# Gathering one operand by accumulating transfers, with two queues trading their loads, in a two-layer adapter kernel

## The chip, the cores and the metric

One Trainium2 chip (trn2), one core. The metric is the device time of one execution in microseconds (us); the figure of a kernel is the median of its runs.

## The reference

32 samples of x, each 64 x 512. Two residual layers follow each other, both conditioned by an index per sample:

```python
def _L0_cond_ref(x, conditions, weights):      # weights: 200 x 64 x 64
    w = weights[conditions]
    return jnp.einsum('bct,bcd->bdt', x, w)

def _L1_cond_ref(x, W, A, Bm, scalings, adapter_idx):   # W 512x512, A 8x16x512, Bm 8x512x16
    H = jnp.einsum('btd,od->bto', x, W)
    xa = jnp.einsum('btd,brd->btr', x, A[adapter_idx])
    delta = jnp.einsum('btr,bor->bto', xa, Bm[adapter_idx])
    return H + delta * scalings[adapter_idx][:, None, None]

x = x + _L0_cond_ref(x, itok_B_1_198, L0_cond_weights)
x = x + _L1_cond_ref(x, L1_cond_W, L1_cond_A, L1_cond_Bm, L1_cond_scalings, itok_B_0_6)
```

All of it is float32.

## The kernel before, in words

Two samples share the 128 partitions, so there are 16 tiles of 128 x 512. For each tile the kernel applies layer 1 first, on the raw x: z = x (W + identity), and beside it u = x A for the two samples of the tile. Layer 0 and its residual are then one product with w0 + identity, where w0 is a 128 x 128 block-diagonal matrix with the two samples' 64 x 64 weights. The low-rank part is v = u (w0 + identity), then v B, added in the same PSUM bank.

The columns of a tile's first product are W's 512 and A's 32 (2 samples x rank 16), 544 in all, split into two PSUM banks of 272. The W bank holds W columns alone, the A bank the other W columns and the 32 of A. Each operand is split into a rounded high part (ScalarE, fp32r) and a low part (VectorE, the difference), and a bank is twelve matmuls: high x high, low x x high, and high x x low W, for each of four blocks of K (`PRODUCTS`, `products`). Tiles 0 and 1 (`PLAIN = 2`) don't do that: their banks are plain fp32 products of unrounded operands, four for a bank (`plain_products`), recorded as two matmuls each. Their A columns are copied by ScalarE, scaled, into both ends of `w_late` (`take_raw_a`, `RAW_A`). For later tiles all eight adapters' A are scaled once, rounded and split into `a_table`, and GpSimd casts the two samples' columns from it into `moving` (`take_a`): even tiles at one end, odd tiles at the other.

Each engine has its order of work written out by hand; engines wait for each other through semaphores only. The queues before the change are:

- SyncE (SP): the index list, head_b, head_d, w_late, then for each tile x (`load_x`), the two 64 x 64 blocks of w0 (`load_w0`, 16 KB each, line 232) and, from tile 6 on, the store of the tile six before.
- GpSimd: the identity, a memset of all of `w0_sb` (line 302), then B's rows for each tile (`load_b`, line 290: two transfers of 128 KB, each row of B to four partitions, waiting for the buffer four tiles before), an addition of the identity to w0 (`add_identity`, line 299; one tile at a time for tiles 0 and 1, later two tiles at once, at odd tiles), and `take_a` (line 283).
- ScalarE: head_a, head_c and a_scales are asked for; then high parts of W, x, z, B, v and w0, the copies of z for tiles 0 and 1 and the copies of the output. `high_of_w0` (line 400) for tiles 2 and 3 stands between `take_z(1, A_PART)` and `high_of_v(1)`.
- VectorE: the identity's additions to W's diagonal, then the low parts and the mask of u by sample (`take_low_rank`).
- TensorE: the W banks of tiles 0 and 1, W bank of tile 2 in between, A bank of tile 0, `weigh_low_rank(0)` (v, line 685), A bank of tile 1, `plain_layer0(0)` (line 702 and the B product, line 696), `weigh_low_rank(1)`, A bank of tile 2, `plain_layer0(1)`, `weigh_low_rank(2)` (line 688), and from tile 3 on a loop: A bank, two thirds of the W bank, layer 0 of the tile before (lines 709, 710, 696, 714), v, and the last third of the W bank.

In the profile w0_sb and w0_parts are shown as w_sb and w_parts.

Of the kernel before, what the change touches and what calls it, by code (L numbers as in the profile page):

```python
# [6 lines left out]
def adapted_residual_kernel(nc, xt, heads, w0, head_a, head_b, head_c, head_d, w_late_t, a_t, b_t, out):  # L7
# [20 lines left out]
    GROUPS = 4  # L28
# [22 lines left out]
    RAW_A = (AC + LATE, 0)  # L51


    HH, HL, LH = 0, 1, 2
    PRODUCTS = [(n, k) for n in (HH, LH, HL) for k in range(K)]

# [13 lines left out]
            (HEAD_AT[3] + X_HALF, HEAD_AT[3] + 2 * X_HALF))  # L70

# [11 lines left out]
    with ctx:  # L83
# [14 lines left out]
        head = sb("head", [P, HEAD_AT[-1]], fp32)  # L98
        w_late = sb("w_late", [P, K, AC + LATE + AC], fp32)
# [37 lines left out]
        w0_cleared = sem("w0_cleared")  # L137
# [13 lines left out]
        w0_added = sem("w0_added")  # L151
# [27 lines left out]

        def x_block(t, k):  # L180

            at = X_AT[t][k // (K // 2)] + k % (K // 2) * P
            return head[:, at:at + P]

        def x_of(t):

            return head[:, X_AT[t][0]:X_AT[t][0] + WIDTH] if t < EARLY else x_raw[:, t - EARLY, :]

        def w_rows(p):

            (c0, _), (k0, k1) = PIECES[p]
            if c0:
                return w_late[:, k0:k1, AC:AC + LATE]
            return head[:, W_AT[p]:W_AT[p] + 2 * HALF].rearrange("p (k n) -> p k n", k=K // 2)

        def w_block(k, c0, c1):

            if c0 >= HALF:
                return w_late[:, k, AC + c0 - HALF:AC + c1 - HALF]
# [18 lines left out]
        def z_part(t, part):  # L218
            bank = bank_of(t, part)
            at, col, n = Z_PARTS[side(t)][bank]  # L220
            if t < PLAIN and part == A_PART and RAW_A[t] == 0:
                at += AC
# [3 lines left out]
        def _(sync):  # L226
# [3 lines left out]
            def load_w0(which, t):  # L230
                for s in range(PER):
                    sync.dma_start(w0_sb[s * C:(s + 1) * C, t, s * C:(s + 1) * C],
                                   w0[ds(which[s], 1), :, :].rearrange("a c d -> (a c) d"),
                                   ).then_inc(w0_loaded[BATCH_OF[t]], 16)
# [9 lines left out]
            sync.dma_start(w_late[:, :, AC:AC + LATE], w_late_t).then_inc(w_late_loaded, 16)  # L244
            sync.wait_ge(index_loaded, 16)
            which = read_indices(sync, 0, 0, w0.shape[0], 2 * READ)
            sync.wait_ge(w0_cleared, 1)
            load_w0(which[0], 0)
            load_w0(which[1], 1)
            load_x(3)  # L250
            load_w0(which[2], 2)
            load_w0(which[3], 3)
            for t in range(4, TILES):
                if t % READ == 0:
                    which = read_indices(sync, 0, t, w0.shape[0], READ)
                load_x(t)
                load_w0(which[t % READ], t)
# [11 lines left out]
        def _(pool):  # L269
# [5 lines left out]
            def take_a(which, t):  # L275

                at = 0 if t % 2 else AC + OUT
# [7 lines left out]
            def load_b(which, t):  # L285

                if t >= BBUFS:
                    pool.wait_ge(b_stack_ready, t - BBUFS + 1)
                for s in range(PER):
                    pool.dma_start(b_raw[s * C:(s + 1) * C, t % BBUFS, :],  # L290
                                   b_t[ds(which[s], 1), :, :].rearrange("a r (g n) -> (a r) g n", g=1)
                                   .to_broadcast([RANK, GROUPS, OUT]),
                                   ).then_inc(b_loaded[t % BBUFS], 16)

            def add_identity(i):
                first, end = BATCHES[i]
                pool.wait_ge(w0_loaded[i], 16 * PER * (end - first))
                every = ident[:].rearrange("p (a q) -> p a q", a=1).to_broadcast([P, end - first, P])
                nc.gpsimd.tensor_tensor(out=w0_sb[:, first:end, :], in0=w0_sb[:, first:end, :], in1=every,  # L299
                                        op=ALU.add).then_inc(w0_added, 1)  # L300
# [25 lines left out]
        def _(act):  # L326
# [5 lines left out]
            first = read_indices(act, 1, 0, ADAPTERS, PLAIN)  # L332
# [13 lines left out]
            def take_raw_a(t):  # L346

                at = RAW_A[t]
# [34 lines left out]
            def high_of_x(t):  # L383
                act.wait_ge(x_loaded[t - 2], 16)
                if t >= PLAIN + XBUFS:
                    act.wait_ge(w_bank_done, t - XBUFS + 1)
                nc.scalar.activation(x_high[:, t % XBUFS, :], x_of(t), ACT.Copy).then_inc(x_high_ready, 1)  # L387
# [9 lines left out]
            def high_of_w0(i):  # L397
                first, end = BATCHES[i]
                act.wait_ge(w0_added, i + 1)
# [429 lines left out]
```

## Time and profile before

| | |
|---|---|
| time, median of 3 runs | 76.97 us (76.96 to 77.12) |
| the profiled execution | 76.68 us, of which 75.0 are the span |
| granted TensorE clock | 1.00, the 2.4 GHz level |
| TensorE (PE) busy | 70.7 us, 94% |
| weight loads (PEld) | 65.4 us, 87% |
| VectorE (DVE) busy | 55.2 us, 74% |
| ScalarE (ACT) busy | 51.3 us, 68% |
| GpSimd (POOL) busy | 32.8 us, 44% |
| DMA | 14.55 MB, mean 194 GB/s over the span |

Times are counted from the start of the span. L12 is line 12 of the kernel. Register work, branches and the issuing of transfers by SP and ACT are not counted as busy; the time in which GpSimd makes the descriptors of its transfers is. Matmuls overlap, and the end of one is modelled; the chain that ended last gives each only the time by which it moved the chain on.

### The profile page before, as it was taken

The page shows a single profiled execution, that of the slowest core. Times are in us where ns is not written, and L with a number is a line of the kernel's source. Part 1 is how long each engine was busy: PE and PEld are TensorE (multiplying, and loading weights), DVE is VectorE, ACT ScalarE, POOL GpSimd, SP SyncE. Part 2 cuts the span into 40 slices and gives each one's busy share as a digit, 9 for nine tenths or more (in the row PEclk, how much of TensorE's full clock was granted, in tenths as well). Part 3 has the DMA queues.
Part 4 walks back from the last instruction along what each step waited for, and adds up shares of the span by engine and source line. Part 5 has one row for each costly group of instructions (what it writes and reads, how often), then busy time and mean ns, then how long its engine had stood idle before and what let it go on. Part 6 is the DMA issues. An engine that isn't in the chain of part 4 may idle for free.

```text
span 75.0 us, 1943 instructions
## 1 busy us (share of the span) xinstructions
PE 70.7 (94%) x468; PEld 65.4 (87%) x468; DVE 55.2 (74%) x143; ACT 51.3 (68%) x126; POOL 32.8 (44%) x76
## 2 busy tenths in 40 slices
PE   5999899999999999999999999999999999999940
PEld 5996689786999999999999999999999999999930
DVE  3019499897989877979797959797797949765920
ACT  0733888957988686977668666867696867566440
POOL 5700399997846282556245620690258320000000
PEclk9999999999999999999999999999999999999999
DMA  0999378786678757978968675578326430303025
GB/s 0 290 389 380 87 227 231 209 253 194 187 246 285 254 166 234 253 217 294 334 211 294 223 261 143 141 212 282 120 62 220 140 144 0 140 13 140 0 100 179
DMA packets 9677, 14.55 MB, mean 194 GB/s; under 512 B 3650, under 2 KB 4418, under 8 KB 9666
## 3 DMA queue, kind: packets, MB, share of 16 engines
q1 hardware_dynamic: 7554, 9.16, 37.5%
q0 software_dynamic: 1536, 4.20, 18.4%
q10 hardware_dynamic: 576, 1.07, 4.1%
q8 instruction: 4, 0.07, 0.4%
q14 instruction: 7, 0.06, 0.3%
HBM read 10.23 MB, written 4.19 MB: 192 GB/s over the span
## 4 chain that ended last, share of the span: by engine, by line
PE 86%; DMA 8%; SPq 1%; DVE 1%; issue 0%
PE z_ps L654 56%; DMA head<-head_d 8%; PE z_ps L642 6%; PE out_ps L696 5%; PE out_ps L709 4%; PE out_ps L710 4%; PE out_ps L714 4%; PE v_ps L688 2%; PE out_ps L702 2%; DVE out_sb L629 1%; PE v_ps L685 1%; SPq L242 0%; SPq L241 0%; PE v_ps L714 0%; PE v_ps L710 0%
## 5 line engine op out<-in xcount | busy, mean ns | idle before, releaser
L654 PE MATMUL z_ps<-moving,x_high 128*128 128x272 f32 x224 | 33.2, 288 | 0.0
L654 PEld LDWEIGHTS z_ps<-moving,x_high 128*128 128x128 f32 x224 | 29.8, 188 | 0.7 <-ACT z_plain L373 0.2
L290 POOL DMA_DIRECT2D b_raw<-b_t x32 | 16.2, 508 | 14.4 <-DMA a_scales<-a_t 5.4
L654 PE MATMUL z_ps<-moving,x_low 128*128 128x272 f32 x112 | 18.8, 289 | 0.0
L654 PEld LDWEIGHTS z_ps<-moving,x_low 128*128 128x128 f32 x112 | 15.8, 188 | 0.1
L511 DVE TENSOR_TENSOR z_low<-z_ps,z_high 128x272 fp32r<-128x272 f32 (+1 forms) x28 | 11.8, 422 | 1.2 <-ACT z_high L364 0.2
L283 POOL CAST moving<-a_table 128x128 fp32r x28 | 8.0, 316 | 10.5 <-PE z_ps L654 10.5
L520 DVE TENSOR_TENSOR b_stack<-b_raw,b_high 128x512 fp32r<-128x512 f32 x16 | 11.5, 718 | 0.4 <-ACT b_high L380 0.4
L380 ACT ACTIVATE b_high<-b_raw,group_sb 128x512 fp32r<-128x512 f32 x16 | 11.5, 716 | 0.0
L394 ACT ACTIVATE v_high<-v_ps,group_sb 128x128 fp32r<-128x128 f32 x16 | 5.9, 366 | 7.8 <-PE v_ps L688 7.8
L364 ACT ACTIVATE z_high<-z_ps 128x272 fp32r<-128x272 f32 (+1 forms) x28 | 10.5, 376 | 0.5 <-PE z_ps L654 0.3
L488 DVE TENSOR_TENSOR x_low<-x_raw,x_high 128x512 fp32r<-128x512 f32 x13 | 9.8, 757 | 0.1
L413 ACT ACTIVATE out_sb<-out_ps 128x512 f32<-128x512 f32 x15 | 8.8, 590 | 0.5 <-PE out_ps L714 0.5
L387 ACT ACTIVATE x_high<-x_raw 128x512 fp32r<-128x512 f32 x13 | 8.3, 637 | 0.0
L409 ACT ACTIVATE low_rank_parts<-own_low_rank 128x96 fp32r<-128x96 f32 x14 | 4.0, 284 | 5.9 <-DVE own_low_rank L540 5.9
L299 POOL TENSOR_TENSOR w_sb<-w_sb,ident 128x256 f32<-128x256 f32 (+1 forms) x9 | 6.9, 769 | 2.5 <-DMA w_sb<-w 2.4
L696 PE MATMUL out_ps<-b_stack,v_stack 128*128 128x512 f32 (+1 forms) x16 | 7.0, 435 | 0.0
L546 DVE TENSOR_TENSOR low_rank_parts<-own_low_rank,low_rank_parts 128x32 fp32r<-128x32 f32 x14 | 3.2, 227 | 4.9 <-ACT low_rank_parts L409 4.9
L709 PE MATMUL out_ps<-z_high,w_parts 128*128 128x512 f32 (+1 forms) x14 | 5.4, 388 | 0.0
L710 PE MATMUL out_ps<-z_high,w_parts 128*128 128x512 f32 (+1 forms) x14 | 5.4, 383 | 0.0
L714 PE MATMUL out_ps<-z_low,w_parts 128*128 128x512 f32 (+1 forms) x14 | 5.4, 382 | 0.0
L560 DVE SCALAR_TENSOR_TENSOR v_stack<-v_ps,group_sb,v_rest 128x128 fp32r<-128x128 f32 x14 | 4.9, 351 | 0.5
(58 smaller groups left out, 77.1 us busy)
## 6 DMA issues: line engine op xcount, KB each, us to landing
b_raw<-b_t POOLq DMA_DIRECT2D x32, 128.0 KB, 3.2
out<-out_sb SPq DMA_DIRECT2D x15, 256.0 KB, 3.2
x_raw<-xt SPq DMA_DIRECT2D x13, 256.0 KB, 3.7
w_sb<-w SPq DMA_DIRECT2D x32, 16.0 KB, 3.2
w_late<-w_late_t SPq DMA_DIRECT2D x1, 480.0 KB, 6.9
head<-head_c ACTq DMA_DIRECT2D x1, 400.0 KB, 4.2
head<-head_d SPq DMA_DIRECT2D x1, 384.0 KB, 6.1
head<-head_a ACTq DMA_DIRECT2D x1, 264.0 KB, 2.9
```

What stands on the lines that cost most here:

```text
L290: pool.dma_start(b_raw[s * C:(s + 1) * C, t % BBUFS, :], b_t[ds(which[s], 1), :, :].rearrange("a r (g n) -> (a r) g n", g=1) .to_broadcast ...
L364: nc.scalar.activation(z_high[:, t % 2, col:col + n], z, ACT.Copy).then_inc(z_high_ready[part], 1)
L380: nc.scalar.activation(b_high[:, t % 2, :], b_raw[:, t % BBUFS, :], ACT.Copy, scale=group_sb[:, LOW_B:LOW_B + 1]).then_inc(b_high_ready, 1)
L413: nc.scalar.activation(out_sb[:, t, :], out_ps[t % 2][:], ACT.Copy).then_inc(out_ready, 1)
L488: nc.vector.tensor_tensor(out=x_low[:, t % XBUFS, :], in0=x_of(t), in1=x_high[:, t % XBUFS, :].bitcast(fp32), op=ALU.subtract).then_inc(x_ ...
L511: nc.vector.tensor_tensor(out=z_low[:, t % 2, col:col + n], in0=z, in1=z_high[:, t % 2, col:col + n].bitcast(fp32), op=ALU.subtract).then_ ...
L520: nc.vector.tensor_tensor(out=b_stack[:, t % 2, :], in0=b_raw[:, t % BBUFS, :], in1=b_high[:, t % 2, :].bitcast(fp32), op=ALU.subtract).th ...
L654: last = nc.tensor.matmul(z_bank(t, part), x[:, t % XBUFS, k * P:(k + 1) * P], moving[:, int(n == HL), k, at:at + HALF], start=((n, k) == ...
L696: return nc.tensor.matmul(dst, v_stack[:, t % 2, :], b_stack[:, t % 2, col:col + n], start=False, stop=stop)
L709: nc.tensor.matmul(dst, w0_parts[:, t, 0, :], z_high[:, t % 2, col:col + n], start=True, stop=False)
L710: nc.tensor.matmul(dst, w0_parts[:, t, 1, :], z_high[:, t % 2, col:col + n], start=False, stop=False)
L714: return nc.tensor.matmul(dst, w0_parts[:, t, 0, :], z_low[:, t % 2, col:col + n], start=False, stop=True)
```

## The change

- w0 is no longer cleared, loaded by SyncE and then increased by the identity on GpSimd. VectorE copies the identity into all of `w0_sb` at the start (two instructions, `w0_preset`), and GpSimd asks for transfers that add w0's blocks to it (`add_w0`, `accum_op=ALU.add`), for tiles 4 and up two tiles at once, at even tiles. Waits for `w0_added` become waits for the transfers (`w0_loaded`).
- B's rows are asked for by SyncE (`load_b` moved), with x of tile 4 ahead of B of tile 3.
- Tile 1's A bank is computed from rounded parts: x tile 1 is rounded and split (`high_of_x(1)`, `low_of_x(1)`), GpSimd casts its A columns from `a_table` (`take_a` of tile 1), and the bank is twelve matmuls with the low part of x last (`LOW_X_LAST`). `a_table` is made ahead of W's last two pieces, and tile 2's `take_a` waits for tile 1's bank, since both use the same columns.
- VectorE and ScalarE get a new order around it.

```diff
         @block.sync
-            which = read_indices(sync, 0, 0, w0.shape[0], 2 * READ)
-            sync.wait_ge(w0_cleared, 1)
-            load_w0(which[0], 0)
-            load_w0(which[1], 1)
+            which = read_indices(sync, 1, 0, ADAPTERS, 2 * READ)
+            load_b(which[0], 0)
+            load_b(which[1], 1)
             load_x(3)
-            load_w0(which[2], 2)
-            load_w0(which[3], 3)
+            load_b(which[2], 2)
+            load_x(4)
+            load_b(which[3], 3)
             for t in range(4, TILES):
                 if t % READ == 0:
-                    which = read_indices(sync, 0, t, w0.shape[0], READ)
-                load_x(t)
-                load_w0(which[t % READ], t)
+                    which = read_indices(sync, 1, t, ADAPTERS, READ)
+                if t > 4:
+                    load_x(t)
+                load_b(which[t % READ], t)
...
         @block.gpsimd
             def take_a(which, t):
-                at = 0 if t % 2 else AC + OUT
+                at = 0 if t % 2 and t > 1 else AC + OUT
+                if t == 2:
+                    pool.wait_ge(plain_bank_done[1], 1)
...
+            def add_w0(which, t):
                 for s in range(PER):
+                    pool.dma_start(w0_sb[s * C:(s + 1) * C, t, s * C:(s + 1) * C],
+                                   w0[ds(which[s], 1), :, :].rearrange("a c d -> (a c) d"),
+                                   accum_op=ALU.add).then_inc(w0_loaded[BATCH_OF[t]], 16)
...
-            nc.gpsimd.memset(w0_sb[:], 0.0).then_inc(w0_cleared, 1)
-            pool.wait_ge(ident_ready, 1)
             pool.wait_ge(index_loaded, 16)
-            which = read_indices(pool, 1, 0, ADAPTERS, 2 * READ)
-            pool.wait_ge(a_loaded, 16)
-            load_b(which[0], 0)
-            load_b(which[1], 1)
-            add_identity(0)
-            add_identity(1)
-            load_b(which[2], 2)
+            rows = read_indices(pool, 0, 0, w0.shape[0], 2 * READ)
+            pool.wait_ge(w0_preset, 2)
+            add_w0(rows[0], 0)
+            add_w0(rows[1], 1)
+            which = read_indices(pool, 1, 1, ADAPTERS, READ + 1)
             pool.wait_ge(a_ready, 1)
-            take_a(which[2], 2)
-            load_b(which[3], 3)
-            add_identity(BATCH_OF[3])
-            take_a(which[3], 3)
+            take_a(which[0], 1)
+            add_w0(rows[2], 2)
+            add_w0(rows[3], 3)
+            take_a(which[1], 2)
+            take_a(which[2], 3)
             for t in range(4, TILES):
                 if t % READ == 0:
+                    rows = read_indices(pool, 0, t, w0.shape[0], READ)
                     which = read_indices(pool, 1, t, ADAPTERS, READ)
-                else:
-                    add_identity(BATCH_OF[t])
-                load_b(which[t % READ], t)
+                    add_w0(rows[0], t)
+                    if t + 1 < TILES:
+                        add_w0(rows[1], t + 1)
                 take_a(which[t % READ], t)
...
         @block.scalar
             take_z(1, W_PART)
+            act.wait_ge(a_scaled_ready, 1)
+            nc.scalar.activation(a_table[:, :, 0, :], a_scaled[:], ACT.Copy).then_inc(a_high_ready, 1)
             high_of_w(2)
             high_of_w(3)
-            take_raw_a(1)
-            act.wait_ge(a_scaled_ready, 1)
-            nc.scalar.activation(a_table[:, :, 0, :], a_scaled[:], ACT.Copy).then_inc(a_high_ready, 1)
+            high_of_x(1)
             take_z(0, A_PART)
...
         @block.vector
+            for first, end in ((0, 2 * READ), (2 * READ, TILES)):
+                every = ident[:].rearrange("p (a q) -> p a q", a=1).to_broadcast([P, end - first, P])
+                nc.vector.tensor_copy(w0_sb[:, first:end, :], every).then_inc(w0_preset, 1)
...
-            low_of_w(2)
-            low_of_w(3)
-            dve.wait_ge(own_rank_ready, 2 + PER)
-            take_low_rank(0)
             dve.wait_ge(a_high_ready, 1)
             nc.vector.tensor_tensor(out=a_table[:, :, 1, :], in0=a_scaled[:],
                                     in1=a_table[:, :, 0, :].bitcast(fp32),
                                     op=ALU.subtract).then_inc(a_ready, 1)
+            low_of_w(2)
+            dve.wait_ge(own_rank_ready, 2 + PER)
+            take_low_rank(0)
+            low_of_w(3)
+            low_of_x(1)
+            low_of_v(0)
             low_of_z(2, W_PART)
-            low_of_v(0)
             low_of_b(0)
...
         @block.tensor
             weigh_low_rank(0)
-            pe.wait_ge(raw_cols_ready, 2 * PER)
-            plain_products(1, A_PART, without_diagonal_first).then_inc(plain_bank_done[1], 1)
+            pe.wait_ge(w_high_ready, len(PIECES))
+            pe.wait_ge(a_cols_ready, PER)
+            products(1, A_PART, LOW_X_LAST).then_inc(plain_bank_done[1], 1)
             plain_layer0(0)
             weigh_low_rank(1)
-            pe.wait_ge(w_low_ready, len(PIECES))
             a_bank(2)
```

## Rows read from the trace of the kernel before

**Rows 1.** The chain that ended last, in order of time: start, us, what.

```profile
1.71 6.11 DMA head<-head_d
...
12.64 1.84 PE z_ps L642 x8
14.48 0.86 PE out_ps L702 x2
...
15.79 1.50 PE z_ps L654 x12
...
18.15 0.23 PE out_ps L696
18.38 0.15 PE v_ps L688
```

**Rows 2.** Busy time by stretch: PE, PEld, DVE, ACT, POOL; clock, DMA, GB/s.

```profile
7.00:7.50 0.50, 0.42 (x2) 0.00 (x0) 0.50 (x1) 0.00 (x0) 0.00 (x0) 1.00 1.11 388
...
22.00:70.00 48.00, 48.00 (x349) 46.05 (x348) 38.88 (x102) 34.98 (x89) 18.64 (x45) 1.00 0.59 190
```

**Rows 3.** The timeline from 14.9 to 23 us: start, us, engine, line, operation.

```profile
14.90 1.06 POOL L299 TENSOR_TENSOR w_sb<-w_sb,ident 128x256 f32<-128x256 f32 x1
...
15.29 1.23 DVE L520 TENSOR_TENSOR b_stack<-b_raw,b_high 128x512 fp32r<-128x512 f32 x1
...
15.91 0.99 POOL L283 CAST moving<-a_table 128x128 fp32r x2
16.00 0.42 ACT L400 ACTIVATE w_parts<-w_sb 128x256 fp32r<-128x256 f32 x1 [0.82 <-POOL w_sb L299]
...
16.70 0.29 DVE L556 TENSOR_TENSOR v_stack<-v_ps,v_high 128x128 fp32r<-128x128 f32 x1 [0.19 <-ACT v_high L394]
...
17.87 0.22 DVE L546 TENSOR_TENSOR low_rank_parts<-own_low_rank,low_rank_parts 128x32 fp32r<-128x32 f32 x1 [0.35 <-ACT low_rank_parts L409]
...
18.14 0.19 PEld L688 LDWEIGHTS v_ps<-w_parts,low_rank_parts 128*128 128x128 f32 x1 [0.39 <-DVE low_rank_parts L546]
...
22.86 0.41 ACT L400 ACTIVATE w_parts<-w_sb 128x256 fp32r<-128x256 f32 x1
```

**Rows 4.** The timeline from 6 to 13 us.

```profile
6.13 2.48 SPq L232 DMA_DIRECT2D w_sb<-w  x4
...
9.12 0.68 DVE L582 TENSOR_TENSOR a_scaled<-a_scales 128x512 f32<-128x512 f32 x1
...
11.05 1.29 POOL L299 TENSOR_TENSOR w_sb<-w_sb,ident 128x128 f32<-128x128 f32 x2
...
11.27 0.62 ACT L426 ACTIVATE a_table<-a_scaled 128x512 fp32r<-128x512 f32 x1
...
11.92 0.97 DVE L590 TENSOR_TENSOR a_table<-a_scaled,a_table 128x512 fp32r<-128x512 f32 x1
```

**Rows 5.** Groups of instructions, whole span: shapes, count, busy us, mean ns.

```profile
L520 DVE TENSOR_TENSOR b_stack<-b_raw,b_high 128x512 fp32r<-128x512 f32 x16 | 11.5, 718 | 0.4 <-ACT b_high L380 0.4
...
L495 DVE TENSOR_TENSOR moving<-w_late,moving 128x480 fp32r<-128x480 f32 x2 | 1.3, 666 | 0.2 <-ACT moving L343 0.2
...
L537 DVE TENSOR_TENSOR low_rank<-z_ps,own_rank 128x96 f32<-128x96 f32 x2 | 0.5, 258 | 0.1
...
L283 POOL CAST moving<-a_table x28: 292/296/751, 13.3 to 60.8; 128x128 fp32r x28
```

**Rows 6.** Waits in the first 22 us: who, for what, us in total, times, longest.

```profile
DVE head L483 <- DMA head<-head_b: 2.8, 1, 2.8
```

**Rows 7.** GpSimd's B transfers, all 32 (ns); last, the landing of 17.2 us's.

```profile
L290 POOL DMA_DIRECT2D b_raw<-b_t x32: 502/502/637, 8.8 to 58.2; - x32
...
DMA to landing us min/median/max: 2.3/3.2/5.0
...
DMA to landing us min/median/max: 2.5/2.5/2.5
```

**Rows 8.** Landing of SP's w0 transfers, all 32.

```profile
DMA to landing us min/median/max: 1.9/3.2/4.7
```

More of the change, by code:

```diff
@@ L48, in adapted_residual_kernel @@
     BANK_AT = (BANK - HALF, 0)
-    RAW_A = (AC + LATE, 0)
     HH, HL, LH = 0, 1, 2
     PRODUCTS = [(n, k) for n in (HH, LH, HL) for k in range(K)]
+    LOW_X_LAST = [(n, k) for n in (HH, HL, LH) for k in range(K)]
     ROWS = (K - 1, *range(K // 2, K - 1), *range(0, K // 2))
@@ L178, in adapted_residual_kernel, with x_count @@
         A_PART, W_PART = 0, 1
+        def x_count(t):
+            return {2: 1, 1: 2}.get(t, t)
         def x_block(t, k):
@@ L185, in x_of, with x_part @@
         def x_of(t):
+            if t == 1:
+                both = head[:, X_AT[1][0]:X_AT[1][0] + 2 * X1_STEP].rearrange("p (h n) -> p h n", h=2)
+                return both[:, :, 0:X_HALF]
             return head[:, X_AT[t][0]:X_AT[t][0] + WIDTH] if t < EARLY else x_raw[:, t - EARLY, :]
+        def x_part(parts, t):
+            to = parts[:, t % XBUFS, :]
+            return to.rearrange("p (h n) -> p h n", h=2) if t == 1 else to
         def w_rows(p):
@@ L295, in add_identity @@
[L295 to L300, printed above, removed]
-            nc.gpsimd.memset(w0_sb[:], 0.0).then_inc(w0_cleared, 1)
@@ L331, in _ @@
             act.wait_ge(index_loaded, 16)
-            first = read_indices(act, 1, 0, ADAPTERS, PLAIN)
+            first = read_indices(act, 1, 0, ADAPTERS, 1)
             def high_of_w(p):
@@ L398, in high_of_w0 @@
                 first, end = BATCHES[i]
-                act.wait_ge(w0_added, i + 1)
+                act.wait_ge(w0_loaded[i], 16 * PER * (end - first))
                 nc.scalar.activation(w0_parts[:, first:end, 0, :], w0_sb[:, first:end, :],
@@ L486, in low_of_x @@
             def low_of_x(t):
-                dve.wait_ge(x_high_ready, t - PLAIN + 1)
-                nc.vector.tensor_tensor(out=x_low[:, t % XBUFS, :], in0=x_of(t),
-                                        in1=x_high[:, t % XBUFS, :].bitcast(fp32),
+                dve.wait_ge(x_high_ready, x_count(t))
+                nc.vector.tensor_tensor(out=x_part(x_low, t), in0=x_of(t),
+                                        in1=x_part(x_high, t).bitcast(fp32),
                                         op=ALU.subtract).then_inc(x_low_ready, 1)
@@ L531, in take_low_rank @@
                     dve.wait_ge(rank_parts_ready, t - PLAIN)
-                at = 0 if t < PLAIN and RAW_A[t] == 0 else A_AT
-                u = z_ps[t % 2][:, A_BANK[side(t)], at:at + AC]
+                u = z_ps[t % 2][:, A_BANK[side(t)], A_AT:A_AT + AC]
                 if t < PLAIN:
@@ L639, in plain_products @@
                 for n, k in ks:
-                    at = min(RAW_A[t], AC)
-                    w = w_late[:, k, at:at + LATE + AC] if part == A_PART else w_block(k, 0, HALF)
+                    w = w_late[:, k, :] if part == A_PART else w_block(k, 0, HALF)
                     last = nc.tensor.matmul(z_bank(t, part), x_block(t, k), w, start=(n == 0), stop=(n == K - 1))
@@ L649, in products @@
                     x = x_low if n == LH else x_high
+                    if t < PLAIN and (n, k) == (HL, 0):
+                        pe.wait_ge(w_low_ready, len(PIECES))
                     if (n, k) == (HH, 0):
[L651 removed]
+                        pe.wait_ge(x_high_ready, x_count(t))
                     if (n, k) == (LH, 0):
[L653 removed]
+                        pe.wait_ge(x_low_ready, x_count(t))
                     last = nc.tensor.matmul(z_bank(t, part), x[:, t % XBUFS, k * P:(k + 1) * P],
                                             moving[:, int(n == HL), k, at:at + HALF],
[L656 removed]
+                                            start=((n, k) == which[0] if t < PLAIN else (n, k) == PRODUCTS[0]),
+                                            stop=((n, k) == which[-1] if t < PLAIN else (n, k) == PRODUCTS[-1]))
                 return last
             def a_bank(t):
[L660 removed]
+                pe.wait_ge(a_cols_ready, PER * t)
                 if t - 2 < PLAIN:
```

52 lines of the change are left out of this document (23 added, 29 removed).

## Prediction

> **What bounds the kernel now.** I read the chain that ended last first, then the busy time of each engine by stretch, then the timeline of the first 19 us engine by engine, then the landing times of the small transfers.
>
> The chain in order of time [rows 1] is the wait for the transfer of head_d until 7.82 us and, from there, TensorE matmuls with no hole to the end. The windows say the same of the steady part: from 22 to 70 us TensorE is busy for all 48.00 us, GpSimd for 18.64 [rows 2]. So only two things can move the end: less TensorE work, or a stall put into (or taken out of) the matmul chain. The diff changes TensorE's work at one place only, tile 1's A bank, and everything else in it decides who delivers operands, above all between 9 and 18.5 us. That stretch is where I look.
>
> One place there is exactly tight already. Tile 2's low-rank matmul (line 688) stands in the chain at 18.38, behind L696 at 18.15 [rows 1], and its weight load starts at 18.14 [rows 3]. That load waits for a serial run that begins with w0 of tiles 2 and 3: GpSimd's identity add ends at 15.96, ScalarE's rounding L400 starts at 16.00, then v_high, VectorE's v_stack 16.70, w0's low part, own_low_rank, ScalarE's parts, VectorE's low part 17.87 to 18.09, and the load at 18.14. So 2.14 us lie between the start of L400 and that load [rows 3], and before the change it costs about nothing because TensorE is only just ready.
>
> **The change, part by part.** TensorE. Tile 1's A bank was four fp32 products, recorded as eight matmuls, 1.84 us in the chain at 12.64. It becomes twelve fp32r matmuls. The same kind and number stands at 15.79: 1.50 us [rows 1]. Gain 0.34 us, if nothing else stops TensorE before 18.4.
>
> Its operands. GpSimd now needs A's rounded table for tile 1, and a_table is therefore made earlier. a_scaled ends at 9.12 + 0.68 = 9.80 [rows 4] and does not move. ScalarE, which no longer makes tile 1's raw copies of A, is free by then and rounds it in 0.62 [rows 4]: 10.45. VectorE's low part took 0.975 beside a GpSimd add that read SBUF at the same time [rows 4]; alone I take the 0.68 of the other 512-column operation of two SBUF inputs, L582 [rows 4]: 11.2. GpSimd's two casts take 0.54 alone (two of 0.296 overlapping a little [rows 5]) and 0.99 beside a VectorE subtraction [rows 3]. So tile 1's A columns are ready between 11.8 and 12.9, depending on who gets through; I take the middle, 12.3. TensorE wants them at 12.64, so no stall in the middle case and 0.3 in the worst.
>
> The extra rounding of x tile 1 costs ScalarE about 0.62 and VectorE 0.68, as 512 columns did above [rows 4]. ScalarE loses two raw A copies in exchange. VectorE has nothing to give back: counting two pieces of W at 0.666, the mask of tile 0 at 0.258 [rows 5] and x at 0.68 on from 11.2, which is 2.27, less the small overlaps that back-to-back instructions show, x_low(1) is ready at 13.2 to 13.6, and it is wanted for the third group of four matmuls at 12.64 + 1.00 = 13.64. Hidden, barely. b_stack(0), two places on in VectorE's queue, is then due at about 14.5 to 15.0, and is wanted when plain_layer0(0) has run its 0.86, at 14.14 + 0.86 = 15.0. Hidden too, barely.
>
> GpSimd and VectorE beside each other. From 15.29 to 16.52 L520 took 1.23 us where the same instruction takes 0.718 on average, and the cast that began at 15.91 needed 0.75 of the 0.99 [rows 3, 5]; L590 shows the same from the other side [rows 4]. So an overlap of a cast with a subtraction whose two inputs are both in SBUF costs one of them about the other's time. The changed order has two such meetings: take_a(1) with low_of_w(2), and take_a(2) and take_a(3), now back to back, with low_of_b(0) and low_of_x(3). The Trainium skill (SBUF — State Buffer, Who interferes with whom) states this as an exclusive lock between a VectorE instruction with two SBUF inputs and a GpSimd instruction that reads SBUF. By that rule the casts of take_a(1) end at 12.3 to 12.9, without it at 11.85.
>
> w0 by accumulating transfers, tiles 0 and 1. VectorE presets 2048 columns with the identity, between its start-up work and head_b, for which it idled 2.8 us [rows 6]. The copy is not in the trace: four times L582's 0.68 for 512 columns [rows 4] is 2.7 and my upper bound; the lower one is half of that, as it reads one input instead of two. Either fits in 2.8. The transfers go out at about 5 us and land by 10 at the median latency of the B transfers, 3.2 [rows 7]; they are needed at 12.4, before the chain's 12.64 [rows 1]: hidden, at zero. Without those 2 us of cover the chain would shift by whatever they are late. They do share the DMA engines with head_d in a stretch at 388 GB/s [rows 2]: two transfers of 16 KB are under 0.1 us, four counted twice 0.3. I take 0 and keep 0.3 for the range, because it would shift the whole chain, which starts from head_d [rows 1].
>
> w0 of tiles 2 and 3: this is the term that decides. The four transfers are queued behind take_a(1) on GpSimd, so they begin at 12.3. An issue takes 0.51 (502 ns and a gap) [rows 7], if an accumulating one costs no more, so the last begins at 12.3 + 3 × 0.51 = 13.83; I take that as the floor of an issue, and twice as much as the other end (a rival below). From there to landing, B's transfers from GpSimd took 2.3 to 5.0, median 3.2, with 128 KB each; in a calm stretch 2.5 [rows 7]. w0's small ones from SP took 1.9 to 4.7 [rows 8]. No row shows one that accumulates, which needs the old values too. I take 2.5, since the transfer is small and the queues have by then mostly drained (SP's B requests start at 6.13 where its w0 requests did [rows 4]). Landing: 13.83 + 2.5 = 16.33. GpSimd's add is gone, so L400 can start then; ScalarE itself had come to it at 16.00 − 0.82 = 15.18 [rows 3], comes about 0.6 later with x tile 1 in its queue, and waits, with high_of_v(1), take_out(0) and high_of_low_rank(2) behind it. The run of 2.14 puts the weight load of L688 at 18.47 + 0.04 of signalling = 18.51, against 18.14: 0.37 us later. TensorE, which is done 0.34 earlier with everything before it, waits about 0.7 there and the gain is swallowed.
>
> The Trainium skill (DMA: Bandwidth & Descriptors, Latency and other measured facts) gives about 1 us to the first byte for a transfer from GpSimd and 0.6 for one from SP. By that the move of w0 costs it 0.4 us a transfer; the floors of the rows, 2.3 and 1.9, differ by the same.
>
> The rest. B from SP: its queue only waited for stores and has room; B(0) is asked for at 6.13, where w0 was [rows 4], and no longer behind a_scales on GpSimd; zero. load_b(t) now holds SP's later x loads behind b_stack(t-4), but those run two tiles ahead of use. In the steady part GpSimd trades four B issues in two tiles for four of w0, loses an identity add and keeps its casts; with 18.64 of 48 us busy [rows 2] I cost it at zero. w0 of tiles 4 and 5 is issued from about 17.5 on, lands near 22.5 by the median of the B transfers [rows 7], and is rounded at 22.86 [rows 3]: also zero, though by little.
>
> **Sum.** The profiled execution took 76.68 (75.0 of span, 1.68 around it). +0.37 makes it 77.05. The median of the runs shown is 76.97, 0.29 above the profiled one; on it, 76.97 + 0.37 = **77.34**. A measurement of this kernel tells 0.2% (0.15 us) from no change.
>
> **Rivals.**
> *The gain comes through (faster).* If GpSimd's casts slip in before the subtraction (11.85), the last transfer starts at 13.38 and lands in 2.3, at 15.7, then L688's load is due at 17.85 and TensorE, at 18.38 − 0.34 = 18.04, is the bound again: −0.34, 76.63. For it: the transfers are eight times smaller than the B ones I borrow from. Against: the row of L520. It turns at a landing of 15.8. Chance 0.28.
> *A draw.* Landing between 15.8 and 16.1: 76.97. Chance 0.17.
> *Late w0 (my forecast).* Landing from 16.1 to 17.2 (latency up to 3.4, or casts at 12.9): +0.15 to +1.25. Chance 0.43.
> *Accumulating issues are dear.* If each takes 1 us of GpSimd, the last starts at 15.3 and lands at 17.8 to 18.3, and take_a(2) waits behind them until 16.9 where TensorE wants it at about 15.45 (15.79 − 0.34 [rows 1]): +1.9 to +2.3, some 79.0. Nothing in the trace speaks for it or against it. Chance 0.12.
>
> Faster 0.28, same 0.17, slower 0.43 + 0.12 = 0.55. The range goes from the gain in full, 76.6, to a landing at about 17.1 and leaves out the dear issues: 76.6 to 78.1. The likeliest case alone is 77.1 to 78.1.
>
> **What would show it.** In the profile after: twelve L654-type matmuls of about 1.5 us for tile 1's A bank; the two casts for tile 1 stretched over 0.54 and a subtraction beside them; a ScalarE wait for a w0 transfer just before the rounding of tiles 2 and 3, and its end after 16.0; a wait of TensorE's weight load before the first low-rank matmul of tile 2; from there on the same spacing of tiles. I am wrong if the last of the four transfers lands before 15.8, if head_d comes later than 7.8, or if a hole opens in TensorE after 22 us.

## The result, and the profile after

The changed kernel takes 77.47 us (median of 20 runs, 76.85 to 78.5) against 76.97 for the one before in its 20 runs: a ratio of 1.0071, 95% interval 1.0047 to 1.0096, so slower by about 0.55 us. Ratios here and below leave out the executions that were over 1.5% above their kernel's fastest, so they need not equal the quotient of two medians. The forecast was 77.34 and slower. The profiled execution took 77.13, 75.5 of it span, against 76.68 and 75.0.

The chain that ended last, in order of time, of the changed kernel (start, us, what), which answers to [rows 1]:

```profile
1.72 5.39 DMA head<-head_d
...
7.13 0.64 ACT x_high L393
...
8.49 0.61 DVE a_scaled L590
...
9.79 0.70 DVE a_table L594
...
11.97 0.43 POOL w_sb L302
...
13.46 0.43 POOL w_sb L302
...
14.21 1.50 POOL moving L297
...
15.75 1.78 PE z_ps L664 x12
17.53 0.86 PE out_ps L713 x2
18.39 0.23 PE out_ps L707
18.62 0.35 PE v_ps L699
```

From 7 to 15.7 us the chain no longer runs through TensorE. It goes through the high and low parts of tile 2's x, A's scaling and table, GpSimd's issues for w0 (L302) and GpSimd's casts of A columns (L297), and comes back to TensorE at tile 2's A bank. The timeline of the same stretch, answering to [rows 3] and [rows 4]:

```profile
10.67 0.77 POOL L297 CAST moving<-a_table 128x128 fp32r x2 [1.55 <-DVE a_table L594]
...
10.70 0.87 PE L664 MATMUL z_ps<-moving,x_low 128*128 128x272 f32 x4
...
11.38 3.31 POOL L302 DMA_DIRECT2D w_sb<-w  x4
...
13.14 0.67 PE L664 MATMUL z_ps<-moving,x_low 128*128 128x272 f32 x4
...
13.98 2.18 POOL L297 CAST moving<-a_table 128x128 fp32r x4
...
15.75 0.78 PE L664 MATMUL z_ps<-moving,x_high 128*128 128x272 f32 x4 [0.64 <-POOL moving L297]
...
16.53 0.42 ACT L406 ACTIVATE w_parts<-w_sb 128x256 fp32r<-128x256 f32 x1 [1.76 <-DMA w_sb<-w]
...
17.23 0.29 DVE L561 TENSOR_TENSOR v_stack<-v_ps,v_high 128x128 fp32r<-128x128 f32 x1 [1.67 <-ACT v_high L400]
...
18.58 0.19 PEld L699 LDWEIGHTS v_ps<-w_parts,low_rank_parts 128*128 128x128 f32 x1 [0.59 <-DVE low_rank_parts L551]
...
18.81 0.66 PE L664 MATMUL z_ps<-moving,x_high 128*128 128x272 f32 x4
```

Two things are late. The four issues of w0 for tiles 2 and 3 take 3.31 us, 0.83 each, where I had 0.51, and the casts for tiles 2 and 3 stand behind them: TensorE waits 0.64 before tile 2's A bank. And w0's last transfer lands at about 16.5, so ScalarE waits 1.76 with the rounding of w0, and the run of 2.05 us (2.14 before) puts the weight load of tile 2's low-rank matmul at 18.58.

The group of the casts over the whole span (shapes, count, busy us, mean ns, idle before), answering to [rows 5]:

```profile
L297 POOL CAST moving<-a_table 128x128 fp32r x30 | 15.7, 821 | 5.8 <-PE z_ps L664 4.2
```

The preset, among the instructions that touch w0_sb (count, ns min/median/max, first and last start):

```profile
L581 DVE COPY w_sb<-ident x2: 418/685/952, 1.9 to 2.2; 128x512 f32<-128x512 f32 x1, 128x1536 f32<-128x1536 f32 x1
```

A cast's mean went from 316 to 821 ns. A cast behind issues is recorded with its wait: the four of 13.98 begin 0.71 us before the issues ahead of them end (11.38 + 3.31 = 14.69). The steady part did not suffer (stretches, columns as in [rows 2]): TensorE is busy throughout, and from tile 3's A bank to the end of the span it is 56.6 us before and 56.7 after.

```profile
22.00:70.00 48.00, 48.00 (x348) 46.01 (x347) 38.63 (x102) 35.06 (x89) 21.82 (x40) 1.00 0.66 189
```

**A measure that the first loads don't move.** In this execution head_d landed 0.7 us earlier than in the profiled one of before (7.11 against 7.82). To compare traces I therefore count from the first matmul with a low part of x in tile 2's W bank (11.05 in before, 10.70 after), to the first matmul of tile 2's A bank, and from there to that of tile 3's. The three matmuls in before are these:

```profile
11.05 0.87 PE L654 MATMUL z_ps<-moving,x_low 128*128 128x272 f32 x4
...
15.54 0.74 PE L654 MATMUL z_ps<-moving,x_high 128*128 128x272 f32 x4
...
18.36 0.67 PE L654 MATMUL z_ps<-moving,x_high 128*128 128x272 f32 x4
```

All numbers of the first three columns are differences of such starts, each from the one execution that was profiled. The last column has the median and ratio of 12 runs (20 of the changed kernel at first, 6 of the one with all w0 ahead of the casts); the ratios are against the kernel before on the same chip, whose medians were 76.62 to 76.97:

| kernel | to tile 2's A bank | on to tile 3's | sum | median, ratio to before (95%) |
|---|---|---|---|---|
| before | 4.49 | 2.82 | 7.31 | 76.97 |
| before, second trace | 4.50 | 3.32 | 7.82 | 76.85, one run |
| changed | 5.05 | 3.06 | 8.11 | 77.47, 1.0071 (1.0047 to 1.0096) |
| changed, again | 5.04 | 2.86 | 7.90 | 77.48, 1.0066 (1.0029 to 1.0104) |
| tile 2's w0 ahead of the casts | 4.38 | 3.08 | 7.46 | 76.98, 1.0057 (1.0020 to 1.0094) |
| rounded bank, queues of before | 5.10 | 2.96 | 8.06 | 77.77, 1.0090 (1.0052 to 1.0129) |
| queues alone | 4.49 | 2.83 | 7.32 | 76.70, 0.9986 (0.9945 to 1.0026) |
| queues alone, again | 4.50 | 2.82 | 7.32 | 76.87, 0.9996 (0.9966 to 1.0027) |
| transfers without accumulation | 4.37 | 2.86 | 7.23 | 77.10, 1.0031 (0.9991 to 1.0070) |
| all w0 ahead of the casts | 5.34 | 2.83 | 8.17 | 77.78, 1.0150 (1.0094 to 1.0205) |
| VectorE casts tile 1 | 4.39 | 2.83 | 7.22 | 77.75, 1.0100 (1.0064 to 1.0137) |
| issues between casts, GpSimd casts | 5.20 | 3.19 | 8.39 | 77.16, 1.0057 (1.0024 to 1.0089) |
| issues between casts, VectorE casts tile 1 | 4.39 | 2.83 | 7.22 | 76.49, 0.9962 (0.9927 to 0.9997) |
| the same, again | 4.41 | 2.89 | 7.30 | 76.74, 1.0009 (0.9970 to 1.0048) |

### The profile page after: what moved, and what is told of

The parts are those of the page before. It is cut to its first block, busy times and chain, and to the rows that moved or that the text cites. A ratio compares the mean times of both kernels' runs of the same rounds, so it can differ in the third digit from the quotient of the medians.

```text
span 75.5 us, 2008 instructions
## 1 busy us (share of the span) xinstructions
PE 71.0 (94%) x472; PEld 65.7 (87%) x472; DVE 55.8 (74%) x146; ACT 51.6 (68%) x125; POOL 35.8 (47%) x68
## 3 DMA queue, kind: packets, MB, share of 16 engines
q0 software_dynamic: 2560, 0.53, 8.5%
## 4 chain that ended last, share of the span: by engine, by line
PE 75%; DMA 7%; POOL 4%; DVE 3%; issue 3%; ACT 2%; SPq 1%; POOLq 0%
PE z_ps L664 54%; DMA head<-head_d 7%; PE out_ps L707 4%; PE out_ps L720 4%; PE out_ps L721 4%; PE out_ps L725 4%; POOL moving L297 3%; PE v_ps L699 3%; POOL w_sb L302 1%; PE out_ps L713 1%; DVE a_table L594 1%; DVE x_low L494 1%; ACT x_high L393 1%; ACT a_table L429 1%; DVE a_scaled L590 1%
## 5 line engine op out<-in xcount | busy, mean ns | idle before, releaser
L302 POOL DMA_DIRECT2D w_sb<-w x32 | 26.6, 1194 | 19.1 <-issue 19.1
L664 PE MATMUL z_ps<-moving,x_high 128*128 128x272 f32 x232 | 34.6, 289 | 0.6 <-POOL moving L297 0.6
L664 PEld LDWEIGHTS z_ps<-moving,x_high 128*128 128x128 f32 x232 | 30.9, 188 | 1.4 <-POOL moving L297 0.8
L664 PE MATMUL z_ps<-moving,x_low 128*128 128x272 f32 x116 | 19.4, 289 | 0.0
L297 POOL CAST moving<-a_table 128x128 fp32r x30 | 15.7, 821 | 5.8 <-PE z_ps L664 4.2
L664 PEld LDWEIGHTS z_ps<-moving,x_low 128*128 128x128 f32 x116 | 16.4, 188 | 0.1
L494 DVE TENSOR_TENSOR x_low<-x_raw,x_high 128x512 fp32r<-128x512 f32 x13 | 8.9, 683 | 0.1
L707 PE MATMUL out_ps<-b_stack,v_stack 128*128 128x512 f32 (+1 forms) x16 | 6.8, 426 | 0.0
L734 PE MATMUL v_ps<-const-float32-1.0 128*128 128x128 f32 x16 | 3.8, 429 | 0.9 <-PEq L833 0.9
```

Source lines behind the costliest of these rows:

```text
L297: nc.gpsimd.tensor_copy(dst, src.bitcast(fp32)).then_inc(a_cols_ready, 1)
L302: pool.dma_start(w0_sb[s * C:(s + 1) * C, t, s * C:(s + 1) * C], w0[ds(which[s], 1), :, :].rearrange("a c d -> (a c) d"), accum_op=ALU.add ...
L494: nc.vector.tensor_tensor(out=x_part(x_low, t), in0=x_of(t), in1=x_part(x_high, t).bitcast(fp32), op=ALU.subtract).then_inc(x_low_ready, 1)
L664: last = nc.tensor.matmul(z_bank(t, part), x[:, t % XBUFS, k * P:(k + 1) * P], moving[:, int(n == HL), k, at:at + HALF], start=((n, k) == ...
L707: return nc.tensor.matmul(dst, v_stack[:, t % 2, :], b_stack[:, t % 2, col:col + n], start=False, stop=stop)
```

## The experiments

**Tile 2's w0 ahead of tile 1's casts.**

```diff
             add_w0(rows[1], 1)
+            add_w0(rows[2], 2)
             which = read_indices(pool, 1, 1, ADAPTERS, READ + 1)
             pool.wait_ge(a_ready, 1)
             take_a(which[0], 1)
-            add_w0(rows[2], 2)
             add_w0(rows[3], 3)
```

> The changed kernel, with the two accumulating transfers of tile 2 issued right after those of tiles 0 and 1, in the hole of 1.6 us that GpSimd has before A's table is ready, so that only tile 3's two stand between tile 1's casts and tile 2's. Theory (late supply): GpSimd's accumulating issues, 0.83 us each in place of the 0.51 I had assumed, make both tile 2's A columns (15.71) and w0 of tiles 2 and 3 (16.5) late; two of them fewer in that place bring tile 2's columns to about 14.8 and w0 to about 15.3 to 15.8, TensorE's wait of 0.6 before tile 2's A bank goes, and the time falls by 0.5 to 0.9 against the changed kernel, to 76.6 to 77.0. Rival (the loss is in the steady part or in the transfers' contention with the rest): no change, 77.4 to 77.6.

Its GpSimd timeline:

```profile
12.46 1.64 POOL L302 DMA_DIRECT2D w_sb<-w  x2 [0.56 <-issue]
14.34 1.98 POOL L297 CAST moving<-a_table 128x128 fp32r x4 [0.24 <-PE z_ps L664]
```

Now GpSimd waits for TensorE before tile 2's casts, not the other way round, and the table's first column falls from 5.05 to 4.38. That part is as expected. The median, 76.98, is in the expected range, but the ratio, 1.0057, is not clear of the changed kernel's, so the gain is shown in the trace and not in the time.

The second column (3.08 against 2.82) is late w0 by itself, for here tile 2's columns hold TensorE up by 0.2 at most: ScalarE still waited 1.11 us for w0, until 16.25.

**The rounded bank**, on the queues of before. GpSimd's order is `add_identity(0)`, `take_a(1)`, `add_identity(1)`, B of tiles 2 and 3, `take_a(2)`, `add_identity` of tiles 2 and 3, `take_a(3)`. So not the bank alone is changed: in the kernel before, B of tile 3 was issued after `take_a(2)`, here it stands ahead of it.

> The kernel before, with tile 1's A bank from rounded parts alone: B still asked for by GpSimd, w0 by SP, cleared and increased by the identity on GpSimd. Late supply: the bank itself saves TensorE 0.34 us, but w0 of tiles 2 and 3 is rounded at 16.0 as before or a little later, so the run of 2.14 us to tile 2's low-rank matmul ends where it did and the time stays within 0.2 of before, 76.8 to 77.2. Rival (the rounded bank is what costs, through the added work of VectorE and ScalarE): slower than before by 0.4 or more, 77.4.

1.0090, slower: neither theory's mechanism as I had written it. The chain says why:

```profile
13.74 1.01 POOL b_raw L300 x2
...
15.94 0.69 POOL moving L293
...
16.67 1.76 PE z_ps L670 x12
```

and the timeline beside it:

```profile
13.25 2.01 POOL L300 DMA_DIRECT2D b_raw<-b_t  x4
15.22 1.39 POOL L293 CAST moving<-a_table 128x128 fp32r x2
```

It is GpSimd's queue again: tile 2's casts end at 16.6 and TensorE waits 0.69. Two things make them late. They can be cast only when tile 1's bank is done (at 14.67), since the two tiles share the place of their columns, and then B's four issues are still running, until 15.26. And the pair took 1.39 us where it takes 0.54 alone, beside two of VectorE's subtractions (x's low part from 15.09 and b_stack from 15.69). So the run doesn't show what the rounded bank costs by itself, as it has B of tile 3 in the way too.

**The queues and accumulating transfers alone**, tile 1 plain; w0 of tiles 0 to 3 is issued in one go ahead of A's table. Twice. The place in GpSimd's order:

```diff
...
-            add_identity(0)
-            add_identity(1)
+            add_w0(rows[0], 0)
+            add_w0(rows[1], 1)
+            add_w0(rows[2], 2)
+            add_w0(rows[3], 3)
...
```

> The kernel before, with the transfers changed alone: identity preset by VectorE, w0 by accumulating transfers from GpSimd (tiles 0 to 3 in one go, before A's table), B from SP; tile 1's A bank plain as before. Late supply: w0 of tiles 2 and 3 lands at about 13, tile 2's columns are cast at about 13.5, nothing waits, so the same time as before to 0.2, 76.8 to 77.1, with w0's rounding no longer at 16.0 but as soon as ScalarE gets there. Rival (exchanging the queues costs by itself, by contention or by SP's waits in the steady part): 77.3 to 77.6, most of what the whole change lost.

> The queue exchange with accumulating transfers alone, tile 1 plain, once more, because its first ratio (0.9986, from 0.9945 to 1.0026) didn't tell it from before. Late supply: same as before or up to 0.3 under it, 76.6 to 77.0, as GpSimd's identity adds no longer stand beside VectorE's subtractions. Rival (the exchange costs by itself): 77.2 or more.

GpSimd's timeline in the first of the two:

```profile
5.56 6.83 POOL L292 DMA_DIRECT2D w_sb<-w  x8 [3.95 <-issue]
```

0.9986 and 0.9996: the same as before to 0.3%, and 7.32 in the table against 7.31; the first median, 76.70, is 0.1 under the range expected. Exchanging the queues costs nothing that these runs can tell where GpSimd has room, although eight issues take 6.83 us. The rival, 77.2 or more, is out.

**Transfers that don't accumulate.**

```diff
-                                   w0[ds(which[s], 1), :, :].rearrange("a c d -> (a c) d"),
-                                   accum_op=ALU.add).then_inc(w0_loaded[BATCH_OF[t]], 16)
+                                   w0[ds(which[s], 1), :, :].rearrange("a c d -> (a c) d")).then_inc(w0_loaded[BATCH_OF[t]], 16)
```

> The changed kernel with w0's transfers from GpSimd as plain ones, which overwrite the identity's diagonal blocks, so layer 0's residual is left out of the output. Everything else is the same. Late supply with dear accumulation: an issue takes 0.5 us in place of 0.83, tile 2's columns come about 1 us earlier and w0 lands about 1.2 us earlier, and the time is 76.7 to 77.0. If instead the 64 rows of 256 bytes are what makes an issue long, whatever the operation, issues stay at 0.8 and the time at 77.4.

The transfers' own times on GpSimd (ns min/median/max), and their landing:

```profile
L302 POOL DMA_DIRECT2D w_sb<-w x32: 516/518/657, 5.6 to 58.3; - x32
...
DMA to landing us min/median/max: 2.0/2.6/3.7
```

and in the timeline, the first four:

```profile
5.56 2.28 POOL L302 DMA_DIRECT2D w_sb<-w  x4 [3.96 <-issue]
```

The landing with accumulation, in the changed kernel:

```profile
DMA to landing us min/median/max: 2.7/3.5/5.0
```

The same rows of 256 bytes are recorded with 0.518 us, and four issues take 2.28 us, 0.57 each. With accumulation four take 3.31, 0.83 each, so the operation and not the row size adds 0.26 an issue. It also adds 0.9 us to the median time to landing, 3.5 against 2.6. 77.10 is just above the expected range. Its interval (0.9991 to 1.0070) includes 1 but also overlaps the changed kernel's (1.0047 to 1.0096), so in time the run tells it from neither; the table's first column (4.37) tells it from the changed kernel (5.05).

**All w0 ahead of the casts.** `add_w0` of tiles 2 and 3 both stand before `take_a(1)`.

> The changed kernel with all four tiles' accumulating transfers ahead of tile 1's casts on GpSimd. w0 is then certainly early (lands at about 15.2), but tile 1's columns come at 12.4 to 13.0 in place of 11.4, and TensorE has to wait about 0.6 for them before tile 1's bank. If lateness of w0 were the only price of the change, this would give 76.9; if GpSimd's issuing time is the price wherever it is put, the wait comes back in front of tile 1's bank and the time is 77.2 to 77.5.

Its timeline, where the casts of tile 1 and tile 1's bank stand:

```profile
12.91 0.53 POOL L297 CAST moving<-a_table 128x128 fp32r x2 [0.53 <-issue]
...
13.54 1.25 PE L664 MATMUL z_ps<-moving,x_high 128*128 128x272 f32 x8 [0.79 <-issue]
```

The wait came back in front of tile 1's bank, 0.79, and the time was 77.78, above even that range. w0's lateness was not the only price: put here, GpSimd's issues make tile 1's columns late.

**VectorE casts tile 1's columns**, so GpSimd has only issues until tile 1's bank is done; w0 of tiles 2 and 3 is issued right behind that of tiles 0 and 1. In VectorE's order:

```diff
...
+            for s in range(PER):
+                dst = moving[:, :, :, AC + OUT + s * RANK:AC + OUT + (s + 1) * RANK].rearrange("p h k r -> p (h k) r")
+                src = a_table[:, ds(tile_1[0][s], 1), :, :].rearrange("p a h (k r) -> p (a h k) r", k=K)
+                nc.vector.tensor_copy(dst, src.bitcast(fp32)).then_inc(a_cols_ready, 1)
             low_of_w(2)
...
```

> The changed kernel with tile 1's A columns cast by VectorE right after A's table, so that GpSimd issues all eight accumulating transfers of tiles 0 to 3 in one go (5.6 to 12.4) and then waits for tile 1's bank. Late supply: w0 of tiles 2 and 3 lands at about 15.2 and no longer holds ScalarE; tile 2's columns start when tile 1's bank is done and are ready some 0.6 to 1.0 later, in time or late by 0.2. VectorE's two casts cost it about 0.4. The 0.34 of the rounded bank comes through in part: 76.5 to 76.9, that is 0.6 to 1.0 under the changed kernel and at or under the one before. Rival (the loss is VectorE's and ScalarE's added work): no better than the changed kernel or worse, 77.4 to 77.8, as VectorE gets still more.

The timeline of VectorE, GpSimd and TensorE:

```profile
11.25 0.37 DVE L602 CAST moving<-a_table 128x128 fp32r x2 [0.15 <-DVE a_table L595]
...
15.41 1.43 POOL L297 CAST moving<-a_table 128x128 fp32r x3 [0.21 <-issue]
18.79 3.31 POOL L302 DMA_DIRECT2D w_sb<-w  x4 [1.95 <-issue]
21.02 2.93 POOL L297 CAST moving<-a_table 128x128 fp32r x4
...
23.53 0.76 PE L670 MATMUL z_ps<-moving,x_high 128*128 128x272 f32 x4 [0.54 <-POOL moving L297]
```

77.75, where I had expected 76.5 to 76.9. Up to tile 3 the table shows what I wanted (7.22, the shortest). Then the same thing happens later: GpSimd stands 1.95 us, most of it for reading indices, issues four transfers, and TensorE waits 0.54 for tile 4's columns; by its starts, tile 4's A bank comes 1.20 us after the group before it (22.33), where no wait makes that 0.50. With these 0.70 the 7.22 become 7.92, 0.61 above before's 7.31; the ratio of 1.0100 is 0.77 us (0.49 to 1.05). 77.75 lies in the range that I had given the rival, so the time alone would speak for the rival; the trace does not, as VectorE's two casts took only 0.37 and nothing of TensorE's waited for them.

**Both kernels once more.**

> The changed kernel once more, beside the others of this call: 77.3 to 77.6. In its trace the start of TensorE's work on w0-independent banks may differ by some tenths with the landing of the first loads; the wait for tile 2's A columns (0.6 before) and ScalarE's wait for w0 (1.8 before) should be there again, with GpSimd's four issues at 3.3 us. If the loss were chance or lay in the first loads, they would be gone or the time would be that of before.

> The kernel before once more, for a second trace of it: 76.6 to 77.3. It shows how far the landing of head_d and w0's rounding at 16.0 move by themselves from one execution to the next. Late supply expects w0's rounding of tiles 2 and 3 to follow GpSimd's identity add again and TensorE to have no wait before tile 2's A bank.

The changed kernel took 77.48. Its wait before tile 2's A bank is there again (0.65; second trace, 5.04), and so is ScalarE's for w0 (1.28):

```profile
16.87 0.42 ACT L406 ACTIVATE w_parts<-w_sb 128x256 fp32r<-128x256 f32 x1 [1.28 <-DMA w_sb<-w]
...
18.39 0.19 DVE L545 TENSOR_TENSOR own_low_rank<-z_ps,own_rank 128x32 f32<-128x32 f32 x1 [0.20 <-PE z_ps L664]
```

The kernel before took 76.85, as expected, with no wait before tile 2's A bank. But its second trace had something that its first did not show:

```profile
14.52 1.52 DVE x_low L488
...
17.72 0.52 DVE low_rank_parts L546
18.28 0.39 PE v_ps L688
```

That was the chain; the timeline beside it:

```profile
14.44 1.60 DVE L488 TENSOR_TENSOR x_low<-x_raw,x_high 128x512 fp32r<-128x512 f32 x1
...
14.73 0.75 POOL L299 TENSOR_TENSOR w_sb<-w_sb,ident 128x256 f32<-128x256 f32 x1
15.41 1.47 POOL L283 CAST moving<-a_table 128x128 fp32r x2
```

Here x's low part took 1.60 us in place of 0.68, beside an identity add and casts on GpSimd, the chain went through VectorE, and tile 3 came 0.5 later. So the meeting of two-input subtractions with GpSimd's reads held up TensorE in one of the two traces of the kernel before. The change removes one such partner, GpSimd's identity adds; that this is worth anything isn't shown, as the two runs with the queues alone gave 0.9986 and 0.9996.

**Issues between the casts**, w0 of tiles 4 and 5 one tile at a time; first with tile 1's casts on GpSimd, then with them on VectorE, the latter twice. GpSimd's order in the latter:

```diff
...
             take_a(which[0], 2)
+            add_w0(rows[0], 4)
             take_a(which[1], 3)
+            add_w0(rows[1], 5)
+            take_a(which[2], 4)
+            take_a(which[3], 5)
...
```

> The changed kernel with GpSimd's order alone altered: w0 of tiles 0 to 2 first, tile 1's casts, w0 of tile 3, tile 2's casts, and w0 of tiles 4 and 5 one tile at a time between the casts of tiles 3 and 4, so that no cast has more than two accumulating issues in front of it. Late supply: TensorE's wait for tile 2's columns shrinks from 0.65 to about 0.2 (they share their place with tile 1's, so they can't start before tile 1's bank is done), w0 comes about 0.5 earlier, and the time is 76.8 to 77.1, 0.4 to 0.7 under the changed kernel. Rival (the loss is the transfers' contention or the steady part): 77.4 again, since the same transfers and instructions are all there.

> As the version in which VectorE casts tile 1's columns, but with GpSimd's issues for tiles 4 and 5 spread between the casts of tiles 2, 3 and 4. That version lost its gain in one place, tile 4's columns, which stood behind four issues (casts from 21.0 to 23.9, wanted at about 22.9). Late supply: this wait goes, what is left of the rounded bank (0.25 by its starts, less 0.2 of wait for tile 2's columns) and w0 in time give 76.6 to 76.9. Rival: 77.4 or more.

> The version with tile 1's columns cast by VectorE and GpSimd's issues spread between the casts, once more, because its first interval (0.9927 to 0.9997) ends near 1. Late supply: again 76.4 to 76.9 and a ratio under 1, with tile 2's bank 4.4 us after the third group of tile 2's W bank and no wait before tile 2's low-rank matmul that shows in TensorE. Rival (the first time was chance): 76.9 to 77.1.

With casts on GpSimd the first pair took 1.38 us beside VectorE's subtractions, and TensorE waited 0.65 before tile 1's bank:

```profile
11.39 1.38 POOL L297 CAST moving<-a_table 128x128 fp32r x2 [0.69 <-issue]
```

77.16 and 1.0057 miss the expected 76.8 to 77.1. The table's 8.39 is far above what the ratio shows, 0.44 us; the profiled execution, 77.51, was above the median of 77.16. With the casts on VectorE (first of the two traces) TensorE has no wait but the 0.2 of tile 2's columns:

```profile
14.35 0.99 POOL L297 CAST moving<-a_table 128x128 fp32r x2 [1.88 <-PE z_ps L675]
15.28 1.63 POOL L302 DMA_DIRECT2D w_sb<-w  x2
...
18.22 0.67 PE L675 MATMUL z_ps<-moving,x_high 128*128 128x272 f32 x4
```

Its ratios are 0.9962 and 1.0009. The loss of the change is gone: its intervals end at 0.9997 and 1.0048, where the changed kernel's begins at 1.0047. But the first ratio, which was clear of 1 by a hair, did not repeat: I can't claim that it beats the kernel before.

## Why the prediction was right, and where it was not

The direction, the size and the place (supply from GpSimd between 9 and 18.5 us, nothing in the steady part) were right. How near 77.34 came is luck in part, as the points show:

- *TensorE's gain, 0.34.* From tile 0's low-rank matmul to the first of plain_layer0(0) it is 12.26 to 14.31 before and 11.91 to 13.65 after, 2.05 against 1.74: 0.31.
- *Tile 1's columns, no stall.* Right: casts of 0.77 beside VectorE's subtraction (I had 0.54 to 0.99), ready at 11.4, TensorE at 12.05.
- *x_low(1), b_stack(0): hidden, barely.* Hidden, and x_low(1) not barely: it ended at 12.59 and was wanted at 13.14; from the first matmul of plain_layer0(0) to the next low-rank one it is 1.08 after and 1.09 before.
- *An issue at 0.51.* This term was mis-sized: 0.83 with accumulation, 0.57 without. "Accumulating issues are dear" had a chance of 0.12 in my list at 1 us each; the issues went two thirds of the way from 0.51 to that, and tile 2's columns were late as that rival had it.
- *Landing 2.5 after the last issue's start.* 3.0 in the first trace, 2.6 in the second, and 2.1 without accumulation. My landing of 16.33 came out as 16.5 all the same, because tile 1's casts ended, and the four issues began, at 11.4 and not at 12.3. The 0.4 us by which I had each transfer of w0 land later for coming from GpSimd doesn't show: plain ones from GpSimd landed in 2.0 to 3.7, SyncE's before in 1.9 to 4.7 [rows 8].
- *Late w0 as the one wait that swallows the gain.* This step failed in part. w0 was late, by the path named, but a wait stood ahead of it that I had only put under the dear issues: tile 2's columns. From the first matmul of plain_layer0(0) to tile 2's A bank it is 1.23 before and 2.10 after: 0.87 late. They can't be cast before tile 1's bank is done, and it is 1.46, 0.23 late, even where GpSimd stands idle until then (VectorE casting tile 1's). The wait of about 0.7 that I put before tile 2's low-rank matmul was small instead: 0.76 from L707 to L699, where 0.63 is no wait. In the table the columns are 0.56 on the first column; late w0 adds 0.24 in one trace and 0.04 in the other on the second.
- *The two waits lie over each other*, so those shares are not what mending one of them would give. In the first trace VectorE's own_low_rank followed w0's low part without a pause, so w0 alone would have put the load at 18.58 with the columns in time too. In the second own_low_rank had to wait 0.20 for tile 2's A bank, and w0 alone would have given about 16.87 + 2.05 = 18.92 (an estimate) against 19.20. Late w0 alone was thus enough for the whole delay of the first trace, as I had said, and for about half of the second's 0.59 in the table; the columns were a second cause beside it. 77.34 came near 77.47 because the dearer issue and the later landing were balanced by the earlier start.
- *SP's B, the preset, w0 of tiles 4 and 5 at zero.* Right. The queues alone change nothing that their runs can tell, and the preset took 0.42 + 0.95 = 1.37 us, my lower bound. w0 of tiles 4 and 5 was in time in the changed kernel; where it was issued later (VectorE casting, one go) it made tile 4's columns late. GpSimd's steady share rose from 18.64 to 21.82 us of 48 at no cost.
- *Casts and subtractions beside each other.* I named the meetings of take_a(2) and take_a(3) with low_of_b(0) and low_of_x(3) and gave them no price. With tile 1's bank rounded, tile 2's two casts took 1.0 us and more from when they could start (14.69 to 15.71 in the changed kernel, 14.35 to 15.34 with GpSimd idle before them), where they take 0.54 alone and took that in the kernel before. At 0.54 they would be done at 14.89 in the latter and TensorE, ready at about 15.16, would not wait (an estimate), so the 0.23 that is left with GpSimd idle comes from the meeting and the shared place together. It does not explain the result alone: the issues are the larger part, since 2.10 fell to 1.43 with two issues fewer and to 1.44 with issues that don't accumulate, with the meeting in place. No run kept VectorE's subtractions away from these casts.
- *The exclusive lock* that the Trainium skill states (SBUF — State Buffer, Who interferes with whom) fits the casts of 0.77 and the subtraction of 1.60.

What stays open: why accumulation adds 0.26 us to an issue (the 32 transfers made 2560 packets with it and 1024 without, for the same 0.53 MB), how much of the late columns the meetings cost, and the 0.2 to 0.3% between the versions near 1, which 12 runs each don't tell apart. A separate place for tile 1's columns, which might take the wait of 0.23 away, wasn't tried; in this kernel a bank's matmul takes A's columns and W's as one run of columns.

## What to carry to other kernels

Count an engine that only feeds others by its queue, not by its busy share: GpSimd was under half busy (47% of the span) and still held up TensorE, because in one stretch of 6 us its issues, index reads and casts followed one another and two consumers waited at the end of the row. When an edit moves work onto such an engine, list for each instruction there who is waiting for it and by when, past the first consumer too. And where two tiles share an operand's place, the earlier tile's end joins the later one's deadline.

## What the runs showed of the hardware

- An accumulating transfer of 64 rows of 256 bytes occupied GpSimd for 0.83 us (four in 3.31) and landed 2.7 to 5.0 us after its start, median 3.5. A plain one took 0.57 (four in 2.28) and landed in 2.0 to 3.7, median 2.6. The plain ones of B, 64 rows of 2 KB, took 0.50 [rows 7].
- Accumulating, the 32 transfers of w0 made 2560 packets, plain 1024.
- Two GpSimd casts of 0.54 us alone took 0.77 to 1.47 beside VectorE subtractions with two inputs in SBUF.
- A VectorE copy of 1536 fp32 columns from a broadcast identity took 0.95 us, 0.62 ns a column, where a two-input operation of 512 took 0.68, 1.33 ns a column.
- The landing of the first loads moved by itself: the point from which the table counts lay between 10.62 and 11.57 us over the traces, with no order by kernel (10.70 and 11.53 for the same changed kernel). That is more than the whole effect studied, and why traces had to be compared from a later point.
